# Two-layer graph network on one core: tables written straight from x1, kept in DRAM for three blocks, and the first batch of a block moved to the end of its slot

## The reference

```python
def _L0_gnn_ref(V, adj, w1, w2, w3, bias):
    o1 = jnp.matmul((adj == 1).astype(jnp.float32), jnp.matmul(V, w1))
    o2 = jnp.matmul((adj == 2).astype(jnp.float32), jnp.matmul(V, w2))
    o3 = jnp.matmul((adj == 3).astype(jnp.float32), jnp.matmul(V, w3))
    return o1 + o2 + o3 + bias

def _L1_gnn_ref(X, adj, W, b, we1, be1, we2, be2):
    h = X @ W.T + b
    e = (h @ we1 + be1) + (h @ we2 + be2).T
    e = jnp.where(e >= 0, e, 0.01 * e)
    scores = jnp.where(adj > 0, e, -9e15)
    return jax.nn.softmax(scores, axis=1) @ h

x = _layernorm(x + _L0_gnn_ref(x, adj, ...), axis=-1)
x = _layernorm(x + _L1_gnn_ref(x, adj, ...), axis=-1)
```

## Time and profile before

| what | value |
|---|---|
| median of three runs | 1557.63 us |
| the profiled execution | 1559.72 us, its span 1558.1 us |
| PE busy | 1422.6 us (91%) |
| DVE busy | 1092.0 us (70%) |
| ACT busy | 978.1 us (63%) |
| POOL busy | 116.1 us (7%) |
| mean granted TensorE clock | 0.976 |

### The profile page before, as it was taken

How to read it: one execution, slowest core, us unless ns; L and a number is a source line. 1 busy time by engine, 2 the same in 40 slices (tenths; PEclk the granted TensorE clock), 3 DMA queues, 4 the chain that set the end, 5 groups by cost and what they waited for, 6 DMA issues and landing times. The chain is left out here.

```text
span 1558.1 us, 19404 instructions
## 1 busy us (share of the span) xinstructions
PE 1422.6 (91%) x6934; PEld 670.4 (43%) x6934; DVE 1092.0 (70%) x2432; ACT 978.1 (63%) x1534; POOL 116.1 (7%) x154
## 2 busy tenths in 40 slices
PE   0867697989999999999999987999999999999996
PEld 0433243444444444444444433444444444444443
DVE  3677667877877868768778657576667676666663
ACT  1333526457457556456456559787888788788873
POOL 2111011100110100100100021000000000000000
PEclk9999799999999999999999997999999999999998
DMA  9999999993979979967969311000000000100100
GB/s 133 138 126 116 126 110 119 128 114 49 117 96 99 106 69 123 83 68 96 84 67 119 28 62 47 8 28 28 28 28 28 28 28 28 55 28 28 35 1 15
DMA packets 87684, 109.60 MB, mean 70 GB/s; under 512 B 4960, under 2 KB 71072, under 8 KB 87584
## 3 DMA queue, kind: packets, MB, share of 16 engines
q0 software_dynamic: 67584, 67.12, 47.1%
q1 hardware_dynamic: 20000, 41.20, 8.0%
HBM read 296.49 MB, written 13.14 MB: 199 GB/s over the span
## 5 line engine op out<-in xcount | busy, mean ns | idle before, releaser
L1222 PE MATMUL ps<-pos_masks,tables 128*128 128x512 fp8e4 x2048 | 616.4, 383 | 39.2 <-DVE pos_masks L607 32.1
L1004 ACT ACTIVATE neg_masks<-e_row,cols 128x512 int8<-128x512 f32 x816 | 509.7, 708 | 110.9 <-PE ps L1222 46.3
L1222 PE MATMUL ps<-neg_masks,tables 128*128 128x512 fp8e4 x1632 | 492.1, 383 | 0.0
L1180 PE MATMUL ps<-edge_masks,tables 128*128 128x512 fp8e4 (+1 forms) x2048 | 464.1, 385 | 0.0
L1222 PEld LDWEIGHTS ps<-pos_masks,tables 128*128 128x128 f16 x2048 | 200.4, 99 | 285.9 <-issue 49.5
L1180 PEld LDWEIGHTS ps<-edge_masks,tables 128*128 128x128 f16 x2048 | 201.4, 99 | 233.3 <-issue 13.7
L1222 PEld LDWEIGHTS ps<-neg_masks,tables 128*128 128x128 f16 x1632 | 161.3, 99 | 197.7 <-issue 9.0
L605 DVE TENSOR_TENSOR neg_masks<-pos_masks,neg_masks 128x2048 uint16<-128x2048 uint16 x102 | 125.0, 1225 | 91.4 <-ACT neg_masks L1004 88.3
L589 DVE TENSOR_SCALAR edge_masks<-edges 128x512 uint16<-128x512 uint16 x512 | 123.4, 306 | 78.1 <-PE ps L1180 78.1
L589 DVE TENSOR_SCALAR pos_masks<-edges 128x512 uint16<-128x512 uint16 x512 | 114.2, 285 | 88.4 <-PE ps L1222 88.4
L992 ACT ACTIVATE edges<-ps 128x1024 uint8<-128x1024 bf16 x64 | 65.1, 1017 | 172.5 <-PE ps L1189 172.5
(11 more groups left out here) (133 smaller groups left out, 845.0 us busy)
## 6 DMA issues: line engine op xcount, KB each, us to landing
adj_in<-adj POOLq DMA_DIRECT2D x84, 512.0 KB, 12.2
tables<-adj POOLq DMA_DIRECT2D x28, 512.0 KB, 31.2
e_row<-e_scratch SPq DMA_DIRECT2D x34, 256.0 KB, 3.9
edges<-adj POOLq DMA_DIRECT2D x16, 512.0 KB, 11.9
part_scratch<-a_c_rows SPq DMA_DIRECT2D x18, 256.0 KB, 2.5
part_in<-part_scratch SPq DMA_DIRECT2D x18, 256.0 KB, 3.0
edges<-x SPq DMA_DIRECT2D x8, 512.0 KB, 6.6
x_rows<-x SPq DMA_DIRECT2D x8, 512.0 KB, 5.5
```

The costliest lines, as they stand in the source:

```text
L1004: ins = e.activation(gate_bufs[GATE[m]][:, n:n + GR].bitcast(I8), e1row[:, q % 2, :], ACT.Sign, bias=t2[:, JC * c + j:JC * c + j + 1])
L1180: ins = e.matmul(ps[:, h, :], v_hl[:, i, JC * c + j, :], U0[:, n:n + GR].bitcast(kind), start=c == 0 and j == 0 and i == 0, stop=c == NCH ...
L1222: ins = e.matmul(z_bank(q, k), tab[:, c, 2 * k + i, j, :], mask[:, n:n + GR].bitcast(F8A), start=first and j == 0 and i == 0, stop=final a ...
```

## The change

1. **Tables in one step.** `table_products` and the old `high` go. The new `high(S)` on ACT writes the high f16 part straight from x1: for each of two tables eight activations of 128x127 with the factor as scale, and a small one for the column of ones. `low(S)` on DVE becomes for each table eight fused operations (x1 times factor, less the high part) and a small subtraction, where it was one subtraction of 128x1024. `ones_column` on POOL goes.
2. **Tables 4 to 6 early.** They too are made at offset 4 and 5 of their own tail, into the buffers `y_turned` and `x_rows` read as f16. SP stores them in DRAM (two transfers of 512 KB a block, and SP waits for both before the x rows of the next block are loaded), and loads them when layer 0 is done (`table_load`). POOL's work, `x1_again`, and six ACT copies and six DVE subtractions in the slots 66 to 68 go.
3. **`high` has moved**: for the blocks 0 and 1 it stands ahead of `convert` in offset 4, for the later ones behind it, ahead of the fresh batch's `gates`. `low` stands at the end of the slot on DVE. SP no longer waits for the tables of the blocks 0 to 3 before it loads x rows.
4. **Fresh batches last in their slot**: on DVE `masks` of a fresh batch follows `check_and_pack` and both `edge_masks`, on PE the batch follows `turn`.
5. **The last block's sums in two banks**: `o_of(7, 0)` and `o_of(7, 1)` write two PSUM banks, both in slot 65, and `v_of(7, 0)` stands behind the masks of its slot.
6. **Order of late groups**: 2, 3, 0, 1, then 4 to 15 (`LATE`), where it was 0 to 15.

The core of the diff:

```diff
+LATE = [2, 3, 0, 1] + list(range(4, 2 * NS))
...
-    for g in range(2 * NS):
+    for g in LATE:
         segs.append((g, [c for c in range(NS) if c not in seen.get(g, ())]))
...
+STAGED = (4, 5, 6)
...
+def fresh(m):
+    return SLOTS[m] == NCH * (BATCH[m][1] // 2 + 1) + START
...
             def next_rows(S):
                 e.wait_ge(s_er, S + 1)
-                ge(e, s_lo, min(S + 1, 4))
+                if S in STAGED:
+                    for n in range(2):
+                        e.wait_ge(s_lo, S + 1)
+                        e.dma_start(tab_dram[S - 4, n], (yT, xg)[n][:, :, :].rearrange("p a b -> p (a b)"))\
+                            .then_inc(s_tabst, 16)
+                    e.wait_ge(s_tabst, 16 * (2 * (S - 3)))
                 xg_load(S + 1)
...
+            def low(S):
+                for k, f in ((0, bq), (2, dq)):
+                    hi, lo = table_place(S, k), table_place(S, k + 1)
                     e.wait_ge(s_hi, 2 * S + k // 2 + 1)
-                    ins = e.tensor_tensor(tab[:, S, k + 1], src, tab[:, S, k], ALU.subtract)
+                    for t in range(RB):
+                        j = JC * S + t
+                        e.scalar_tensor_tensor(lo[:, t, 0:D - 1], X1[:, t, 0:D - 1], f[:, j:j + 1],
+                                               hi[:, t, 0:D - 1], ALU.mult, ALU.subtract)
+                    ins = e.tensor_tensor(lo[:, :, D - 1], f[:, JC * S:JC * (S + 1)], hi[:, :, D - 1], ALU.subtract)
...
+            def high(S):
+                if S in (2, 3):
+                    e.wait_ge(s_pk, GUEST[S] + 1)
+                e.wait_ge(s_x1, S + 1)
                 e.wait_ge(s_er, S + 1)
                 e.wait_ge(s_bd, 2 * (S + 1))
-                for f, dst in ((bq, yT8), (dq, xg[:, :, :])):
+                for k, f in ((0, bq), (2, dq)):
+                    hi = table_place(S, k)
                     for t in range(RB):
-                        ins = e.activation(dst[:, t, :], X1[:, t, :], ACT.Copy, scale=f[:, JC * S + t:JC * S + t + 1])
-                    ins.then_inc(s_pt, 1)
+                        j = JC * S + t
+                        e.activation(hi[:, t, 0:D - 1], X1[:, t, 0:D - 1], ACT.Copy, scale=f[:, j:j + 1])
+                    e.activation(hi[:, :, D - 1], f[:, JC * S:JC * (S + 1)], ACT.Copy).then_inc(s_hi, 1)
...
 # vector, in the loop over slots
                 for m in at(k):
-                    masks(m)
-                    after(m)
-                for S, off in tails(k):
-                    if off == 5 and (S < 4 or S == NS - 1):
-                        low(S, yT8, xg[:, :, :])
+                    if not fresh(m):
+                        masks(m)
+                        after(m)
...
                     edge_masks(k - 1, 1)
+                for m in at(k):
+                    if fresh(m):
+                        masks(m)
+                        after(m)
...
+                    if off == 4 + min(S, 1):
+                        low(S)
...
 # tensor, in the loop over slots
                 for m in at(k):
-                    batch(m)
-                    after(m)
+                    if not fresh(m):
+                        batch(m)
+                        after(m)
                 if k < K:
                     turn(k)
+                for m in at(k):
+                    if fresh(m):
+                        batch(m)
+                        after(m)
```

More of the change, by code:

```diff
@@ L425, in _ @@
                     q += 1
-            for n in range(3):
-                x1_again(n)
+            for S in STAGED:
+                table_load(S)
             row_of(LOWS)
@@ L808, in _ @@
                 for S, off in tails(k):
[L809 removed]
+                    if off == 2 and S < NS - 1:
                         v_of(S, 0)
                 for m in at(k):
[L812 to L819 removed]
+                    if not fresh(m):
+                        masks(m)
+                        after(m)
                 if 1 <= k <= NCH:
@@ L1103, in _ @@
                         b_d_of(S)
-                    if off == 5 and (S < 4 or S == NS - 1):
-                        high(S, yT8, xg[:, :, :])
-                for n, slot in enumerate(AGAIN):
-                    if k == slot + 2:
-                        e.wait_ge(s_l0, 2 * K)
-                        high(4 + n, xr_b, xr[n])
                 for m in at(k + 1):
@@ L1115, in _ @@
                         sd_of(S)
+                    if off == 4 and S < 2:
+                        high(S)
                 if k < K:
@@ L1122, in _ @@
                         y_of(S)
-                    if off == 4 and (S < 4 or S == NS - 1):
-                        table_products(S)
+                    if off == 4 and S >= 2:
+                        high(S)
                 for m in at(k + 1):
@@ L1268, in _ @@
                 for S, off in tails(k):
-                    if off == 2:
+                    if off == 2 and S < NS - 1:
                         o_of(S, 1)
```

113 lines of the change are left out of this document (46 added, 67 removed).

## The result

The changed kernel took 1577.38 us (median of four runs, 1576.00 to 1580.57), the kernel before, on the same chip, 1558.52 (four runs, 1556.46 to 1560.19). The ratio is 1.0125, with a 95% interval of 1.0103 to 1.0146: slower by 18.9 us. I had given 1575, 1560 to 1590, and 0.84 for slower. The profiled execution took 1578.46 us, its span 1576.5 (18.4 above that of before), the mean granted clock was 0.971.

What follows compares the result with a forecast made beforehand. PE, busy 1422.6 of 1558.1 us, was taken as the bound. Terms 0 + 3.2 + 3.6 + 13.2 + 3.8 - 6.2 = +17.6 us on 1559.7 gave 1577.3, or 1575 as median; range 1560 to 1590, slower 0.84.

Steps and rivals of the forecast that it cites:

- slots 13 and 21: Early fresh batches: some 5 us won after slot 13, lost again in slot 21, so zero; ends 5 gained, 3 lost.
- slot 29, without the clock: Fresh batch of slot 29: ACT's tables, gates and `convert` delay the next product, 3.2 us lost.
- slot 37, without the clock: Fresh batch of slot 37: the masks' chain behind the product delays the next product, 3.6 us lost.
- slots 45, 53, 61, without the clock: Moved fresh batches where PE was fully busy: 4.4 us lost a slot, 13.2 us in all, the largest term.
- slow clock in five fresh batches: Waits in slots 29 to 61: slow clock in two of five, 1.9 us each, 3.8 us lost; ends 0 and 9.5.
- end of layer 0, to the last batch: DVE's chain to the second late batch's masks: 9.7 us less work, 2.4 and 0.5 back, 6.2 gained; ends 2 and 10.
- The chain on DVE: Fresh masks behind the second half of `edge_masks`, which awaits layer 0's product: 4.84 us from product's end to batch.
- the transposes of slot 45: ACT's `convert` of slot 45 ends at 625.1, product at 622.13: PE stands 3.0 us ahead of `turn`.
- Costed at nothing: `low` of blocks 1 to 6, 6 MB of table traffic, late groups' order and ACT's table loads: no cost.
- A: Rival: waits of four fresh slots and 6.2 us at layer 0's end go: 1532, half of it 1545; chance 0.09.
- B: Rival: no difference, early gains and layer 0's end offset PE's loss, under 3 us a slot: 1557 to 1561; chance 0.08.
- C: Rival: fused operations and table stores delay following slots too, 19 us more: 1590 and over; chance 0.08.

Runs made afterwards that it cites:

- e2: Changed kernel with only PE's order put back (fresh batch ahead of the transposes), DVE's fresh masks still last: 1580.78 us, ratio 1.0134.
- e4: Changed kernel with ACT's `convert` ahead of the next slot's gates in slots with a fresh batch: 1576.19 us, ratio 1.0118.
- e5: Kernel before with part 4 alone (fresh batches last on DVE and PE): 1619.31 us, ratio 1.0379.
- e1: Changed kernel with part 4 undone (fresh batches first again on DVE and PE), other parts kept: 1554.53 us, ratio 0.9972.
- e6: e1 with part 5 undone too (one bank for the last block's two sums, old order): 1557.04 us, ratio 0.9973.
- e10: e9 with one bank for the last block's products, as in e6: 1548.53 us, ratio 0.9911.
- e7: e1 with low parts and row sums of blocks 2 to 6 in offset 6, of block 7 in offset 7: 1542.99 us, ratio 0.9889.
- e11: e9 with the late groups in the old order, 0 to 15: 1542.31 us, ratio 0.9880.
- e9: The same kernel as e7, run again as base for later runs: 1542.16 us, ratio 0.9886.

## Why the prediction was right

By its own steps, measured in the profiled execution:

| step | predicted | measured |
|---|---|---|
| slots 13 and 21 | 0 | -0.3 |
| slot 29, without the clock | +3.2 | +3.1 |
| slot 37, without the clock | +3.6 | +3.4 |
| slots 45, 53, 61, without the clock | +13.2 | +12.6 |
| slow clock in five fresh batches | +3.8 | +9.5 |
| end of layer 0, to the last batch | -6.2 | -8.4 |
| small steps between | 0 | -0.4 |
| sum at the last batch | +17.6 | +19.6 |

The measured steps are rounded one by one.

*The chain on DVE* was the cause, and its size came from slot 46 of the old trace. It was predicted as 4.84 us from product to batch and is 4.64, in the slots 37, 45, 53 and 61 of the changed kernel and of e2 and e4, and in slot 45 of e5. e2 and e4 show that it is neither PE's order nor ACT's, e5 that in the slots 45 to 61 the tables have nothing to do with it. On ACT's side the transposes of slot 45 were predicted 3.0 us behind the product and were 2.6 (633.65 - 631.02).

*Slots 13 and 21* came out at zero by the predicted route: two waits became one (7.39 us), 5.7 us were won by slot 15, and slot 21 took them back with a wait of 7.76 us for `convert`. That this was all the order's doing shows in e1, which keeps 12.3 us at slot 22 without it. My range for these slots began at -5; it was a statement on the changed kernel, and says nothing on what parts 1 to 3 are worth there.

*The clock* is the term that was mis-sized: two of five batches at 1.9 us were put in, and all five were slow: 1.91, 1.10, 1.68, 2.35 and 2.50 us over the 6.91 of 32 matmuls. The sum, 9.5, is the upper end that was given. In slot 29 the old trace had it too (8.38 us for 31 matmuls, 8.60 now), but that term was set against the old trace's own 394.44, so the new one counts in full. The 5.7 us that the term lacked were partly made up by the end of layer 0, so the total was nearer than its parts. That these two errors had opposite signs is luck.

*The end of layer 0* gained 2.2 us more than I took. The last wait is not shorter, as I wrote it would be, but longer (8.00 us against 4.61); it is reached so much earlier. The parts that I named for this term, 9.7 us (9.2 on the gates' side) less 2.4 and 0.5, give 6.3 to 6.8, not 6.2. The profiles of e6 and e10 give the banks 4.4 us, 2.8 of them clock, where I had 3.2 inside the sum, and e7 shows that low part and row sum of block 7 ahead of the masks cost 4.4 us of wait.

*Costed at nothing*: the low parts, the traffic of the tables, the order of the groups. All held in the changed kernel. Behind slot 45 the two stores were issued at 641.89 and 642.26 and had landed at 645.81, and the x rows were issued at 645.83; e11 bears out the order. The low parts held only because the batch was late: with the order put back (e1) they cost 5 us in slot 30, 2 in slot 38 and about 1 each in 46, 54 and 62. The prediction named the cover as free time on DVE; it was PE's lateness.

The Trainium skill (VectorE: DVE Perf Modes, the section on the errata, SBUF-src ops) has 58 cycles and the elements for such a piece, an estimate of 0.19 us at 0.96 GHz. The rows show eight in 2.18 us, 0.26 us from start to start: the row of the old trace (0.28) was the better price, and the page's own remark, that the formula is under what single operations take, agrees.

Rivals: A (waits go) failed at its own condition, since the batch never started within 1.5 us of the product's end. B needed a loss under 3 us a slot, and the slots 45, 53 and 61 lost 5.9 to 6.7. C did not happen in the changed kernel, but its mechanism is the one that e1 met once the batches were early again.

The best version found is e7/e9: all parts but the fourth, with the low parts two slots later, 0.989 of before in two sessions (1542.99 and 1542.16 us).

## What to carry to other kernels

Moving work to the end of an iteration on one engine is free only as long as its input isn't made late by the same move: look for what the moved step now stands behind, and whether that depends on the very engine that is to be kept busy (here the masks came to stand behind a buffer that PE's product frees). Take the length of such a chain from a place in the old trace where the same steps already stand in that order. And before an edit is called free because it lies under other work, ask whether that work stays where it is when the rest is repaired: the low parts were hidden by the very delay that was to be removed.

## What the runs showed of the hardware

The clock behind a wait. In these traces TensorE ran part of the 32 matmuls behind a wait at the lower of its two levels (1.2 instead of 2.4 GHz, 31 matmuls in 7.8 to 9.6 us instead of 6.69) after each of the longer waits that I compared (3.42 and 4.61 us in the kernel before, 8.00 after, 3.20 in e1, 3.63 in e9), and after shorter ones sometimes: 2.45 us at 384.67 before had it, 2.63 us in e1 and e9 at the same batch had not; 2.19 us before had not, 2.20 us in e10 had; 2.95 us at 1450.27 in the changed kernel had not, while 2.18 at 1419.31 in e10 had. The two waits of about 2.5 and 1.2 us with 0.6 us of transposes between them had it in each of the slots 45, 53 and 61. A wait of that size should be priced with the clock and without.

VectorE beside GpSimd. The multiplication of x by the e1 weights took 2.92 us at 937.63 while POOL worked (two products of 128x1024 from 936.89 us on, 2.58 and 2.75 us long, where two at 925.44 and 927.42 had taken 1.90 each); in the changed kernel, with POOL idle from 910 to 990 us, it took 1.22 at 957.27. The Trainium skill (GPSIMD Engine Reference, Specifications, the row on SBUF interfaces) says that the two share them and contend where a VectorE instruction has two inputs in SBUF; these rows agree. They do not show when it happens: VectorE's multiplication just before, at 936.49, overlapped POOL's first product for most of its time and took 1.22 us.
